# Transformer tower kernel: order of the input loads, and position rows added by VectorE instead of a one-hot matmul

## The reference, cut to what matters

```
patches = patchify(images, 16)                                  # (16, 36, 768)
h = einsum('bnd,ed->bne', patches, W_proj) + b_proj + pos_emb   # (16, 36, 256)
h = concatenate([broadcast(cls_tok), h], axis=1)                # (16, 37, 256)
h = h + attention(layernorm(h))      # 16 heads, W_qkv, W_out
h = h + ffn(layernorm(h))            # each token goes to the one expert of 8
                                     # with the largest gate; score times its output
```

## Time and profile before

| | us |
|---|---|
| three runs | 195.72, 196.68, 396.79 |
| median | 196.68 |
| span of the profiled execution, first to last instruction | 193.6 |
| PE busy in that span | 149.7 (77%) |
| DVE busy | 81.2 (42%) |
| ACT busy | 50.5 (26%) |
| POOL busy | 30.9 (16%) |
| bytes moved | 26.99 MB, mean 139 GB/s |

### The profile page before, as it was taken

The page is one execution under the profiler, slowest core; times in us unless marked ns, Lnnn a source line. Parts: engine busy times, 40 slices in busy tenths (PEclk is TensorE's granted clock), DMA queues, the critical chain, the costliest instruction groups (busy, mean ns, idle before and its releaser), DMA issues.

```text
span 193.6 us, 2570 instructions
## 1 busy us (share of the span) xinstructions
PE 149.7 (77%) x937; PEld 121.8 (63%) x937; DVE 81.2 (42%) x243; ACT 50.5 (26%) x137; POOL 30.9 (16%) x41
## 2 busy tenths in 40 slices
PE   0006999898499999999984540188999999999980
PEld 0005688676357676686673430178999999999960
DVE  0011002876966678767885348714212022022030
ACT  0002001409513442424432010007421421431400
POOL 1010001496000001001011100430030430420222
PEclk9999999999999999999999655559999999999999
DMA  6999999300000000100681110240059999940000
GB/s 190 372 361 372 377 377 381 107 3 0 0 0 0 2 3 2 54 3 0 186 301 58 56 54 0 71 145 4 0 181 344 352 318 335 349 156 0 18 19 24
DMA packets 15696, 26.99 MB, mean 139 GB/s; under 512 B 2253, under 2 KB 11012, under 8 KB 15552
## 3 DMA queue, kind: packets, MB, share of 16 engines
q1 hardware_dynamic: 12624, 21.89, 32.5%
q0 software_dynamic: 1024, 2.71, 4.2%
q10 hardware_dynamic: 2032, 2.19, 3.4%
HBM read 24.86 MB, written 2.36 MB: 141 GB/s over the span
## 4 chain that ended last, share of the span: by engine, by line
PE 73%; DVE 10%; DMA 8%; issue 2%; ACTq 2%; ACT 2%; POOL 1%; POOLq 0%; DVEq 0%
PE ps L652 16%; PE ps L664 14%; PE ps L515 8%; PE ps L462 8%; DMA bqk<-b_qk 6%; PE ps L532 5%; PE ps L558 4%; PE ps L544 3%; PE ps L606 3%; PE ps L495 3%; PE ps L460 2%; DVE wide L740 2%; DMA early<-hz_scratch,growu 2%; PE ps L535 2%; PE ps L640 1%
## 5 line engine op out<-in xcount | busy, mean ns | idle before, releaser
L652 PEld LDWEIGHTS ps<-early,w1s 128*128 128x128 f32 x256 | 31.7, 203 | 2.2 <-issue 1.9
L652 PE MATMUL ps<-early,w1s 128*128 128x128 f32 x256 | 32.0, 287 | 1.3 <-DVE early L879 1.3
L664 PE MATMUL ps<-w2s,early 128*128 128x256 f32 x128 | 28.8, 379 | 0.0
L431 ACT ACTIVATE early<-ps,b1s 128x128 f32<-128x128 f32 x64 | 18.2, 371 | 31.8 <-PE ps L652 31.8
L664 PEld LDWEIGHTS ps<-w2s,early 128*128 128x128 f32 x128 | 23.8, 190 | 2.9
L952 POOL DMA_INDIRECT out<-early,srowu x8 | 8.1, 1008 | 49.0 <-DVE early L892 49.0
L462 PE MATMUL ps<-early 128*128 128x256 f32 x60 | 14.9, 414 | 0.0
L887 DVE TENSOR_TENSOR ysum<-ps,b2s 128x256 f32<-128x256 f32 x8 | 3.4, 425 | 26.7 <-PE ps L664 26.7
L462 PEld LDWEIGHTS ps<-early 128*128 128x128 f32 x60 | 12.5, 211 | 2.6 <-issue 0.7
L395 ACT ACTIVATE probs<-shifted 101x296 f32<-101x296 f32 x16 | 7.2, 451 | 24.8 <-DVE shifted L762 24.8
L879 DVE COPY early<-ps 128x256 f32<-128x256 f32 x8 | 3.4, 425 | 22.7 <-PE ps L640 22.7
(11 more groups left out here) (125 smaller groups left out, 196.3 us busy)
## 6 DMA issues: line engine op xcount, KB each, us to landing
w1s<-w SPq DMA_DIRECT2D x8, 1024.0 KB, 5.3
w2s<-w SPq DMA_DIRECT2D x8, 1024.0 KB, 9.4
early<-embed_in SPq DMA_DIRECT2D x6, 448.0 KB, 8.9
hz_scratch<-hz SPq DMA_DIRECT2D x5, 256.0 KB, 2.3
b2s<-b ACTq DMA_DIRECT2D x1, 1024.0 KB, 19.9
wqkv<-w_qkv SPq DMA_DIRECT2D x1, 768.0 KB, 13.0
cf<-const_f ACTq DMA_DIRECT2D x1, 642.0 KB, 11.2
wout<-w_out SPq DMA_DIRECT2D x1, 256.0 KB, 13.4
```

The source lines that it names most:

```text
L431: nc.scalar.activation(gt[:, t % 2, f, :], ps[:, 2 * (t % 2) + f // 4, (f % 4) * P:(f % 4 + 1) * P], ACT.Gelu, bias=b1t[:, f:f + 1]).then_ ...
L652: m = nc.tensor.matmul(ps[:, 2 * (t % 2) + f // 4, (f % 4) * P:(f % 4 + 1) * P], w1s[:, r, k, f * P:(f + 1) * P], xt[:, t % 2, k, :], star ...
L664: m = nc.tensor.matmul(ps[:, 4 + t % 2, 0:D], gt[:, t % 2, f, :], w2s[:, r, f, :], start=(f == 0), stop=(f == FT - 1))
```

## The change

The loads are asked for in another order and from other engines. The one-hot matmul with `sel` and `tab` is gone; in its place stand `pos` (128x5x256, the class token or the position row of each token, 640 KB), `bproj` (the bias, copied to all partitions, 128 KB) and a 0/1 column `patch` in `cf`. DVE forms bias x patch + position in place, five instructions, and then adds the PSUM tile to it, which writes `h`; ACT's copy is gone. The `iota` row leaves `cf` (now 132.5 KB) and is a load of its own. PE starts with slice 0, transposes the gate weights behind slice 0 and multiplies them behind slice 1.

```diff
@@ SP
             for k in range(KE):
                 sp.dma_start(emb[:, k, :], embed_in[k]).then_inc(loaded_emb[k], 16)
+            sp.dma_start(pos[:, :, :], places_in).then_inc(q["loaded_pos"], 16)
             sp.dma_start(wqkv[:, :, :], w_qkv.rearrange("(k p) n -> p k n", p=P)).then_inc(q["loaded_wqkv"], 16)
+            sp.dma_start(cb[:, :], cb_d).then_inc(q["loaded_cb"], 16)
             sp.dma_start(wout[:, :, :], w_out.rearrange("(k p) n -> p k n", p=P)).then_inc(q["loaded_wout"], 16)
...
-            for t in range(RING - 1):
-                load_expert(t)
+            load_expert(0)
+            sp.dma_start(bout[:, :], b_out.partition_broadcast(P)).then_inc(q["loaded_bout"], 16)
+            load_expert(1)
+            sp.dma_start(iota[:, :], iota_d.partition_broadcast(P).rearrange("p o n -> p (o n)"))\
+              .then_inc(q["loaded_iota"], 16)
+            sp.dma_start(b1s[:, :, :], b1.rearrange("e p f -> p e f")).then_inc(q["loaded_b1"], 16)
+            sp.dma_start(b2s[:, :, :], b2.partition_broadcast(P)).then_inc(q["loaded_b2"], 16)
+            load_expert(2)
@@ ACT
-            act.dma_start(sel[:, :], sel_d).then_inc(q["loaded_sel"], 16)
-            act.dma_start(tab[:, :], table).then_inc(q["loaded_tab"], 16)
+            act.dma_start(wgs[:, :], wg).then_inc(q["loaded_wg"], 16)
             act.dma_start(cf[:, :], cf_d).then_inc(q["loaded_cf"], 16)
-            act.dma_start(wgs[:, :], wg).then_inc(q["loaded_wg"], 16)
             act.dma_start(wredt[:, :], w_red_t).then_inc(q["loaded_wred"], 16)
-            act.dma_start(cb[:, :], cb_d).then_inc(q["loaded_cb"], 16)
+            act.dma_start(bproj[:, :], b_proj.partition_broadcast(P)).then_inc(q["loaded_bproj"], 16)
             act.dma_start(bqk[:, :], b_qk).then_inc(q["loaded_bqk"], 16)
             act.dma_start(bv[:, :], b_v).then_inc(q["loaded_bv"], 16)
-            act.dma_start(bout[:, :], b_out.partition_broadcast(P)).then_inc(q["loaded_bout"], 16)
-            act.dma_start(b1s[:, :, :], b1.rearrange("e p f -> p e f")).then_inc(q["loaded_b1"], 16)
-            act.dma_start(b2s[:, :, :], b2.partition_broadcast(P)).then_inc(q["loaded_b2"], 16)
-
-            for j in range(NT):
-                act.wait_ge(q["embedded"], j + 1)
-                nc.scalar.activation(h[:, j, :], ps[:, j, 0:D], ACT.Copy).then_inc(q["h_saved"], 1)
@@ PE
-            pe.wait_ge(q["g_ready"], 1)
-
-            pe.wait_ge(q["loaded_sel"], 16)
-            pe.wait_ge(q["loaded_tab"], 16)
-            for j in range(NT):
-                nc.tensor.matmul(ps[:, j, 0:D], sel[:, j * P:(j + 1) * P], tab[:, :], start=True, stop=False)
...
             for k in range(KE - 3):
                 pe.wait_ge(loaded_emb[k], 16)
                 for j in range(NT):
                     embed(k, j)
+                if k == 0:
+                    pe.wait_ge(q["wgn_ready"], 1)
+                    nc.tensor.transpose(ps[0:16, BZ, 0:E], wgn[:, :], ident[0:E, 0:E]).then_inc(q["wgnt_ps"], 1)
+                if k == 1:
+                    pe.wait_ge(q["wgnt_ready"], 1)
+                    pe.wait_ge(q["loaded_wred"], 16)
+                    for c in range(KD):
+                        m = nc.tensor.matmul(ps[:, BZ, 16 + c * E:16 + (c + 1) * E], wredt[:, c * P:(c + 1) * P],
+                                             wgnt[:, :], start=True, stop=True)
+                    m.then_inc(q["g_ps"], 1)
@@ DVE
+            dve.wait_ge(q["loaded_cf"], 16)
             dve.wait_ge(q["loaded_wg"], 16)
...
+            dve.wait_ge(q["loaded_bproj"], 16)
+            dve.wait_ge(q["loaded_pos"], 16)
+            for j in range(NT):
+                V.scalar_tensor_tensor(pos[:, j, :], bproj[:, :], C("patch")[:, j:j + 1], pos[:, j, :],
+                                       ALU.mult, ALU.add).then_inc(q["pos_ready"], 1)
             for j in range(NT + 1):
                 if j < NT:
+                    dve.wait_ge(q["embedded"], j + 1)
+                    dve.wait_ge(q["pos_ready"], j + 1)
+                    V.tensor_tensor(h[:, j, :], ps[:, j, 0:D], pos[:, j, :], ALU.add).then_inc(q["h_saved"], 1)
                     dve.wait_ge(q["h_saved"], j + 1)
                     norm_stats(h[:, j, :], stats, mv, veps, j, q["veps_ready"])
```

More of the change, by code:

```diff
@@ L70 @@
                   ("valid", NT), ("thr", OVF), ("tri", E * E), ("tilenum", OVF), ("pow", 2),
-                  ("iota", SLOTS)):
+                  ("patch", NT)):
     _F[_name] = (_at, _at + _n)
@@ L108, in constants @@
     put("pow", np.array([[-0.5, 0.5]]))
-    put("iota", np.arange(SLOTS)[None])
+    put("patch", (tok < T) & (tok % S > 0))
     cb = np.zeros((P, NB), np.float32)
@@ L121, in constants, with vit_tower @@
     putb("token", np.stack([tok // 8, tok % 8, np.ones_like(tok)], -1).reshape(P, -1))
[L122 to L130, removed]
+    iota = np.arange(SLOTS, dtype=np.float32).reshape(1, SLOTS)
+    return cf, cb.astype(np.dtype("bfloat16")), iota
+def vit_tower(nc, embed_in, places_in, b_proj, w_qkv, b_qk, b_v, w_out, b_out, wg, w_red_t, w1, b1, w2, b2,
+              cf_d, cb_d, iota_d, out):
     ctx = ExitStack()
@@ L152, in vit_tower @@
         ident = C("ident")
-        sel = sb("sel", [S + 1, TP])
-        tab = sb("tab", [S + 1, D])
+        iota = sb("iota", [P, SLOTS])
+        pos = sb("pos", [P, NT, D])
+        bproj = sb("bproj", [P, D])
         wqkv = sb("wqkv", [P, KD, 3 * D])
@@ L271, in vit_tower @@
         infp = ps[:, 4, 128:128 + 6 * (E + OVF)].rearrange("p (t c) -> p t c", c=6)
-        names = """loaded_sel loaded_tab loaded_cf loaded_cb loaded_wqkv loaded_wout loaded_bqk
+        names = """loaded_pos loaded_bproj loaded_iota pos_ready loaded_cf loaded_cb loaded_wqkv loaded_wout loaded_bqk
             loaded_bv loaded_bout loaded_b1 loaded_b2 loaded_wg loaded_wred
@@ L445, in _ @@
         def _(pe):
[L447 to L454, removed]
-            pe.wait_ge(q["g_ready"], 1)
-            pe.wait_ge(q["loaded_sel"], 16)
-            pe.wait_ge(q["loaded_tab"], 16)
-            for j in range(NT):
-                nc.tensor.matmul(ps[:, j, 0:D], sel[:, j * P:(j + 1) * P], tab[:, :], start=True, stop=False)
             def embed(k, j):
                 return nc.tensor.matmul(ps[:, j, 0:D], emb[:, k, j * P:(j + 1) * P], emb[:, k, TP:TP + D],
-                                        start=False, stop=(k == KE - 1))
+                                        start=(k == 0), stop=(k == KE - 1))
             for k in range(KE - 3):
@@ L485, in _ @@
             HALF = T // 2
+            pe.wait_ge(q["g_ready"], 1)
             for j in range(-(-HALF // P)):
@@ L725, in _ @@
                 .then_inc(q["g_ready"], 1)
+            dve.wait_ge(q["loaded_bqk"], 16)
+            V.tensor_scalar(bqs[:, :], bqk[:, 0:KD], DH ** -0.5, None, ALU.mult).then_inc(q["bqs_ready"], 1)
+            dve.wait_ge(q["loaded_bproj"], 16)
[3 more added lines that the diff above has]
+                                       ALU.mult, ALU.add).then_inc(q["pos_ready"], 1)
             for j in range(NT + 1):
                 if j < NT:
+                    dve.wait_ge(q["embedded"], j + 1)
+                    dve.wait_ge(q["pos_ready"], j + 1)
+                    V.tensor_tensor(h[:, j, :], ps[:, j, 0:D], pos[:, j, :], ALU.add).then_inc(q["h_saved"], 1)
                     dve.wait_ge(q["h_saved"], j + 1)
@@ L820, in places @@
                 for j in range(NT):
-                    m = V.tensor_scalar(place[:, j, c0:c1], C("iota")[:, c0:c1], key[:, j:j + 1], None, ALU.is_equal)
+                    m = V.tensor_scalar(place[:, j, c0:c1], iota[:, c0:c1], key[:, j:j + 1], None, ALU.is_equal)
                 m.then_inc(q["place_ready"], 1)
+            dve.wait_ge(q["loaded_iota"], 16)
             places(0, 2 * P)
@@ L907, in _ @@
                 for j in range(NT):
-                    m = V.tensor_scalar(place[:, j, 0:OVF * P], C("iota")[:, 0:OVF * P], okey[:, 2, j:j + 1], None,
+                    m = V.tensor_scalar(place[:, j, 0:OVF * P], iota[:, 0:OVF * P], okey[:, 2, j:j + 1], None,
                                         ALU.is_equal)
@@ L988 @@
     emb[:, TP:] = a["L0_tok_W_proj"].T
-    table = np.concatenate([a["cls_tok"].reshape(1, D), a["L0_tok_pos_emb"], a["L0_tok_b_proj"].reshape(1, D)])
+    rows = np.concatenate([a["cls_tok"].reshape(1, D), a["L0_tok_pos_emb"]])
+    places = np.zeros((TP, D), np.float32)
+    places[:T] = np.tile(rows, (B, 1))
     bqkv = a["L0_attn_b_qkv"].reshape(3 * KD, P)
-    cf, cb, sel = constants()
+    cf, cb, iota = constants()
     arrays = {
         "embed_in": emb.reshape(KE, P, TP + D),
-        "table": table,
+        "places": places.reshape(NT, P, D).transpose(1, 0, 2),
+        "b_proj": a["L0_tok_b_proj"],
         "w_qkv": a["L0_attn_W_qkv"],
@@ L1007 @@
         "const_bf16": cb,
-        "const_sel": sel,
+        "const_iota": iota,
     }
```

3 lines of the change are left out of this document (removed).

## The result

The changed kernel took 182.12 us (median of four runs, 180.22 to 183.57) beside 196.22 us before (the median of 195.72, 195.75, 196.68 and an outlier of 396.79). The ratio is 0.924, 95% interval 0.919 to 0.930; it is taken over fast runs alone, without the one of 183.57, and is not the quotient of the two medians, 0.928. The forecast was 182.8 us. The profiled execution is the fastest, the one of 180.22 us; its span is 178.3 us, against 193.6 before.

What follows compares the result with a forecast made beforehand. The prediction took the chain behind PE's late embedding start to bound the kernel: tile 0 14.9 us earlier, less 1.0 on DVE, gains 13.9; span 179.7 plus 3.1 gives 182.8 us, range 180.2 to 187.5.

Steps and rivals of the forecast that it cites:

- What bounds the start: Start of the kernel: PE does no embedding before 22.24 us, as `wgs` stands fourth in ACT's list behind 642 KB `cf`.
- Slice 0: First embedding load on SP's queue: forecast to land at 5.3 us, bounds 4.3 and 5.9.
- PE's sum: PE until the first finished tile: load, thirty instructions, slow clock, gate work; tile 0 at 17.0 us, 14.9 earlier.
- Slow start: Embedding's first matmuls on PE at the lower clock level: price 2.5 us, bounds 1.9 and 4.6.
- `pos` on DVE: Five DVE instructions before tile 0, 2.6 us, done 0.7 us ahead of it: cost nothing, bounds 0 and 3 us.
- DVE's pace: Tile normalisation: DVE at 1.63 us per tile against PE's 1.295 gives back 1.0 us, bounds 0.2 and 2.
- The sum: Whole kernel: gain 14.9 - 1.0 = 13.9 us; span 179.7, plus 3.1 to the median, 182.8 us.
- the clock about the experts: Experts' first matmuls: the lower-clock stretch may shift by some 3 us, worth 1.5 us to either side.
- Rival 1: Embedding on PE: slow clock lasts as long as before, price 4.6 instead of 2.5; 184.9 us; chance 0.13.
- Rival 2: Before tile 0: DVE late with `pos`, or its chain stretched by PE's order; up to 3 us, 185.8; shared chance 0.11.
- Rival 4: Loads: SP's queue alone carries much less; 202 us, chance 0.02; milder form 185.1, within a shared 0.11.
- signs of being wrong: Timeline: PE waiting for a slice or `wgn`, L712 on L706, a wait for `wqkv` or `bout`, or a longer later stage.

## Why the prediction was right, point by point

**What bounds the start.** Right: PE waited for its own list while the slices lay there. But the prediction took `wgs` to be late for the 642 KB ahead of it. The runs put some 3 us of the lateness of ACT's list on the 38-row loads: with 48 rows `cf` lands 3.2 us sooner with all its bytes, `wgs` is there at 10.00 instead of 13.09, and in the reordered list 48 rows gain 5.3 us in the median (196.96 to 191.63). The rest of the 13.09 us stays with 48 rows and is gone once `wgs` is first in the list (used at 2.13 us in the run with the loads reordered). By the changed kernel's own design the question did not arise, since `sel` and `tab` are gone; so the sum held, with a cause missing from it.

**Slice 0.** 5.3 us was taken, within 4.3 to 5.9; it came at 3.91 us, below the lower bound. The sum let slice 0 wait for all of ACT's 0.29 MB and added the lag of 1.1 us from before. Neither came: it landed 3.1 us after its issue, ahead of `cf`, which came at 6.6 us. Slice 5 landed 9.2 us after its issue, by 12.4 us (11.8 forecast), `pos` at 13.9 (13.6).

**PE's sum.** Slow start: 2.5 taken. The row of 3.97 us for slice 0 against 2.16 at full pace puts it at 1.8; the gate's work took 0.17 + 0.61 in place of 1.2, and PE waited 0.5 us for `wgn`, which was held to be covered: slice 0 was done at 7.9 us, earlier than assumed, and the gate's chain ended at 8.3, later than the 7 assumed, since `cf` was late. PE's tile 0: about 15.1 us instead of 17.0, nearly all from slice 0 and the slow start.

**`pos` on DVE.** Costed at nothing, with 3 us as the upper bound. This is the term that was mis-sized the other way: PE was 1.9 us earlier and `pos` 0.3 later, so `pos` is what tile 0 waits for, 0.8 us. The five instructions took 2.07 us (2.6 estimated).

**DVE's pace.** 1.52 us per tile, 1.63 forecast; tile 4's L694 started 7.8 us behind tile 0, 8.2 forecast, 7.19 before. It was 3.80 us long beside the clearing, as forecast, and the 1.0 us given back is 0.4 at the keys. By the prediction's own rows it should have been 0.8: before, PE's first group ended 11.2 us behind tile 0, and 12.0 is 0.8 later, not 1.0.

**The sum.** 16.0 us at tile 0 against 14.9, 15.3 us in span against 13.9. The forecast time is closer than its parts, and that is luck: the span is 1.4 us shorter than the 179.7 forecast, while the median lies 3.8 us above the span and not 3.1. Each run takes 1.8 to 1.9 us more than its own span; the rest is scatter between runs, which the prediction took over from the kernel before. It allowed 1.5 us to either side for the clock about the experts. The run with the clock held throughout (0.993 to 0.998 in all six) has a scatter of 0.3 us, so nearly all of the changed kernel's scatter goes with the clock. DVE's slower pace is not shown to be its cause. It does leave PE lightly busy earlier, 3.03 of 4 us from 35 to 39 us before and 2.35 of 4 from 19 to 23 us now, but the kernel before scatters by 5.4 us, and the one with 48 rows and ACT's copies, where DVE does not set the pace, by 3.4 (181.87 to 185.25).

**The rivals.** Rival 1 (long slow start) did not occur. Rival 2 holds in a small part, 0.8 us. Rival 4 (SP's queue alone carries too little) fell: 380 GB/s from 14 to 26 us. Two of the prediction's own signs of being wrong did occur, a wait for `wgn` and L712 behind L706, for 0.5 and 0.8 us.

The parts do not add: loads alone nothing clear, program alone 7.4 us, both 15.3 beside the 197.38 of that group. With 48 rows, one step behind the other: loads 5.3; the order on PE and DVE 8.8 more (191.63 to 182.82); the position rows on DVE 0.7 more, which is within the scatter. PE's order alone is not worth 8.8 us. In the reordered kernel with 48 rows the embedding starts at 18.34 us, with the gate first in the changed kernel at 9.13; of the 9.2 us between them 2.6 are DVE's wait for `bqk`, 2.0 a later start of the gate's chain (`cf` landed later), and 4.6 the one-hot matmuls at the lower clock. No run moves DVE's `bqk` instruction alone. Behind slice 1, with the clock high, the ten one-hot instructions take 2.42 us: there the matmul is cheap, and with 38 rows its loads are what costs.

## What to carry to other kernels

When a small load lands late, look at the row counts of the loads ahead of it in its list as well as at their bytes, and try another row count, as 48 for 38 here. When a part of a change gains nothing, or little, by itself, look for the wait that it leaves in place: here `bqk` in the gate's chain and `wgn` behind slice 0. And when an edit makes another engine set PE's pace, compare the granted clock over all runs, not in the profiled one alone; cheap matmuls in PE's waits, sized to end before the awaited data, bought 4.5 us here by the medians (about 4 by the two ratios) and took nearly all of the scatter away.

## What was not expected of the hardware

A load of 38 rows and 38 KB landed 12.4 us after its issue where one of 48 rows and 48 KB took 7.2, and held up 2 KB behind it (12.8 against 7.7 us). Mean granted clocks of 0.906 to 0.931 in the same program go with spans from 181.7 to 178.3 us. A DVE instruction of 0.41 us took 3.80 beside a POOL clearing of 3.73, and eight DVE instructions took 3.59, 4.15 or 5.20 us with 0.1, 0.8 or 1.8 us of POOL's addition beside them. One wait stays open: in the changed kernel DVE's first L733 began 0.42 us after its operands were there by the rows, where before its like began at once; nothing in the profile names a releaser, and no run tried it.
